# Row maxima of an attention kernel: transposed by VectorE in blocks of 32 and placed by eight small transfers, in place of a matmul and a copy; router fed from sums of both halves

## The reference

```python
# attention (4 heads of 64 channels, n = 1024 pixels)
xn  = group_norm(x, 32 groups) * gn_w + gn_b
q,k,v = split(qkv_w @ xn + qkv_b)
p   = softmax(q^T k / 8, over the keys);   x = x + proj_w @ (v p^T) + proj_b
# conditional convolution (8 experts)
rw  = sigmoid(mean_over_pixels(x) @ router_w.T + router_b)
W1,W2,W3 = sum_e rw[e] * experts_e         # 1x1, 3x3, 1x1
y = relu(bn1(conv1(x))); y = relu(bn2(conv2(y))); out = relu(bn3(conv3(y)) + x)
```

## Time and profile before

| | |
|---|---|
| median of 3 runs | 1910.57 us (1909.94 to 1910.65) |
| the profiled execution, its own time | 1913.63 us |
| its span, first to last instruction | 1911.8 us |
| mean granted TensorE clock | 0.993 of full speed |
| busy: PE / PEld / DVE / ACT / POOL | 97% / 55% / 54% / 57% / 75% |
| packets of all DMAs under 512 B | 26112 of 96673 |

### The profile page before, as it was taken

One profiled execution on the slowest core, in us unless ns is written; L12 is line 12 of the kernel. 1 busy time (PEld: TensorE's weight loads), 2 busy tenths in 40 slices (PEclk: granted clock), 3 DMA queues, 4 the chain that ended last, 5 costly groups with the idle time before them and its releaser, 6 DMA issues.

```text
span 1911.8 us, 29495 instructions
## 1 busy us (share of the span) xinstructions
PE 1846.7 (97%) x8332; PEld 1061.0 (55%) x8332; DVE 1041.8 (54%) x1820; ACT 1084.0 (57%) x1501; POOL 1438.7 (75%) x829
## 2 busy tenths in 40 slices
PE   6899999999999999999999999999999999999986
PEld 4455556555555555555555555555555555565532
DVE  6656556464654646555464654646556465564514
ACT  4455646556465555756556565565655556465452
POOL 3677968778796886968778687786968879687582
PEclk9999999999999999999999999999999999999998
DMA  3022423314233233332324233233332324222233
GB/s 114 27 56 67 117 79 89 96 56 121 88 94 85 65 106 89 105 89 74 100 64 122 76 91 94 65 107 94 94 95 72 89 83 118 76 84 78 64 107 99
DMA packets 96673, 166.72 MB, mean 87 GB/s; under 512 B 26112, under 2 KB 26880, under 8 KB 96640
## 3 DMA queue, kind: packets, MB, share of 16 engines
q1 hardware_dynamic: 96640, 166.31, 30.5%
HBM read 97.41 MB, written 17.04 MB: 60 GB/s over the span
## 4 chain that ended last, share of the span: by engine, by line
PE 87%; DVE 5%; issue 3%; POOL 2%; ACT 2%; DMA 0%; DVEq 0%; SPq 0%; POOLq 0%; ACTq 0%
PE PV L790 23%; PE R L627 14%; PE S L772 12%; PE R L754 11%; PE S L775 10%; PE R L678 5%; PE R L717 4%; DVE mx L994 3%; PE R L670 2%; POOL psum_p L601 2%; PE R L725 2%; PE R L701 1%; PE R L683 1%; DVE K L1015 1%; ACT K L883 1%
## 5 line engine op out<-in xcount | busy, mean ns | idle before, releaser
L601 POOL TENSOR_TENSOR psum_p<-psum_p,prob 128x1024 f32<-128x1024 f32 x384 | 915.7, 2385 | 305.8 <-ACT prob L868 286.6
L994 DVE TENSOR_REDUCE mx<-R 128x1 f32<-128x512 f32 x1006 | 653.5, 683 | 582.6 <-PE R L754 575.5
L868 ACT ACTIVATE prob<-S 128x1024 f32<-128x1024 f32 x512 | 518.3, 1022 | 319.2 <-PE S L775 316.3
L790 PE MATMUL PV<-prob,V 128*64 128x512 f32 x2048 | 469.4, 600 | 0.0
L772 PE MATMUL S<-Q,K 128*128 128x512 f32 x1024 | 445.1, 435 | 2.5 <-ACT prob L868 2.5
L775 PE MATMUL S<-Q,K 128*128 128x512 f32 x1024 | 403.2, 394 | 2.4 <-DMA Q<-mrow 2.4
L754 PE MATMUL R<-K,Q 128*128 128x512 f32 x1006 | 336.5, 405 | 13.1 <-DVE mx L994 7.9
L790 PEld LDWEIGHTS PV<-prob,V 128*64 128x64 f32 x2048 | 135.9, 137 | 254.8 <-issue 239.3
L772 PEld LDWEIGHTS S<-Q,K 128*128 128x128 f32 x1024 | 192.9, 188 | 131.5 <-issue 82.1
L754 PEld LDWEIGHTS R<-K,Q 128*128 128x128 f32 x1006 | 186.0, 187 | 94.1 <-DVE mx L994 49.0
L775 PEld LDWEIGHTS S<-Q,K 128*128 128x128 f32 x1024 | 193.5, 189 | 47.1 <-issue 14.4
(11 more groups left out here) (158 smaller groups left out, 1780.3 us busy)
## 6 DMA issues: line engine op xcount, KB each, us to landing
ex<-in_experts_dram SPq DMA_DIRECT2D x122, 352.0 KB, 3.3
xin<-in_x_dram SPq DMA_DIRECT2D x64, 256.0 KB, 3.2
K<-K SPq DMA_DIRECT2D x128, 128.0 KB, 2.3
Q<-Q SPq DMA_DIRECT2D x128, 128.0 KB, 2.3
x<-in_x_dram SPq DMA_DIRECT2D x64, 256.0 KB, 3.7
rz<-z_dram SPq DMA_DIRECT2D x126, 128.0 KB, 2.9
out_dram<-y SPq DMA_DIRECT2D x63, 256.0 KB, 2.7
V<-v_next SPq DMA_DIRECT2D x16, 512.0 KB, 3.8
```

The source lines that it names most:

```text
L601: nc.gpsimd.tensor_tensor(acc, first_in, prob[:, s % PBUF, :, :], ALU.add).then_inc(add_done, 1)
L790: last = nc.tensor.matmul(PV[own(a), :], V[:, b // NH, kt, a * D:a * D + D], prob[:, s % PBUF, a, :], start=(kt == 0), stop=(kt == KT - 1))
L868: nc.scalar.activation(prob[:, s % PBUF, :, :], S[:, s % 2, :, :], ACT.Exp, scale=D ** -0.5).then_inc(exp_done, 1)
L994: nc.vector.reduce_max(mx[:, b % 2, nh, m:m + 1], R[:, fill_bank(b, m, nh), :], AX.X).then_inc(max_read, 1)
```

## The change

Per block, the matmul, its PSUM bank and the copy are gone. VectorE's `max_of_block` now goes on itself: it writes the eight maxima into the first eight columns of mx1 (now 128 x 32, the rest zeros), waits for that, and transposes each block of 32 x 32 into mxt. The maxima of queries 32g to 32g+31 of query tile t then lie on partition 32g+t, so SP places them with eight DMAs a block (four groups g for each of two heads), each of four pieces of 32 numbers. The sign moves into K2, which holds minus ones. SP's `rows` moves from the tables of jobs to LOADS, at the end of n = 2, 10, 18 and 26, where before it stood at the start of n = 3, 11, 19 and 27. Two banks of FILL_BANKS at n = 8 are swapped. For the router VectorE adds the two halves into pool2 after the last projection, and the router is two matmuls in place of four.

```diff
-    PLACES ... 3: [("row", 0, 1)], 11: [("row", 0, 2)], 27: [("row", 1, 0)];  EARLY 19: [("row", 0, 3), ("v", 1, 2)]
+    PLACES, EARLY: the same without row
-LOADS = {3: [("v1", 0, 0)], 14: [("xin", 2, 0)], ...
+LOADS = {2: [("row", 0, 1)], 3: [("v1", 0, 0)], 10: [("row", 0, 2)], 14: [("xin", 2, 0)], 16: [("xin", 2, 1)], 18: [("row", 0, 3)],
+         19: [("xin", 2, 2), ("xin", 2, 3)], 22: [("h", -1, 0)], 26: [("row", 1, 0)]}
...
-        mx1 = sb("mx1", [P, 2 * QT])
-        mrow = sb("mrow", [2 * QT, P], F32R)
+        mx1 = sb("mx1", [P, ZP])
+        mxt = sb("mxt", [P, ZP])
...
             def rows(i, b):
-                sp.wait_ge(read["row"], BLOCKS * i + b + 1)
+                sp.wait_ge(max_turned, BLOCKS * i + b + 1)
                 for a in range(2):
                     r = 64 - 64 * a
-                    sp.dma_start(Q2[r:r + 1, 2 * p + a, px(hf)].bitcast(F32),
-                                 mrow[QT * a:QT * a + QT, :].bitcast(F32)).then_inc(rows_loaded, 16)
+                    for g in range(QT):
+                        sp.dma_start(Q2[r:r + 1, 2 * p + a, px(hf)].rearrange("o (t g c) -> o g t c", t=QT, g=QT)[:, g, :, :].bitcast(F32),
+                                     mxt[ZP * g + QT * a:ZP * g + QT * a + QT, :]).then_inc(rows_loaded, 16)
...
-                fills += [(K2[r:r + 1, h, :].bitcast(F32), 1.0)]
+                fills += [(K2[r:r + 1, h, :].bitcast(F32), -1.0)]
...
-                elif kind == "row":
-                    pe.wait_ge(max_ready, BLOCKS * i + f + 1)
-                    last = nc.tensor.matmul(bank[0:2 * QT, 0:P], mx1[:, :], negeye[:, :], start=True, stop=True)
...
                 elif kind == "router":
-                    pe.wait_ge(read["proj"], 4 * i + 4)
+                    pe.wait_ge(pooled, i + 1)
                     for c in range(CC):
-                        for hf in range(NH):
-                            last = nc.tensor.matmul(bank[:, 0:E], pool4[:, c, hf:hf + 1].to_broadcast([P, P]), wr[:, c, :],
-                                                    start=(c + hf == 0), stop=(c + hf == CC + NH - 2))
+                        last = nc.tensor.matmul(bank[:, 0:E], pool2[:, c:c + 1].to_broadcast([P, P]), wr[:, c, :], start=(c == 0), stop=(c == CC - 1))
...
             def max_of_block(i, b):
                 dve.wait_ge(max_read, 2 * (32 * i + 8 * b + 8))
-                wait(dve, filled["row"], BLOCKS * i + b)
-                nc.vector.reduce_max(mx1[:, :], mx[:, b % 2, :, :].rearrange("p n m -> p m n"), AX.X).then_inc(max_ready, 1)
-            def row(i, b, bank):
-                wait(dve, rows_loaded, 32 * (BLOCKS * i + b))
-                nc.vector.tensor_copy(mrow[:, :], bank[0:2 * QT, 0:P]).then_inc(read["row"], 1)
+                wait(dve, max_turned, BLOCKS * i + b)
+                nc.vector.reduce_max(mx1[:, 0:2 * QT], mx[:, b % 2, :, :].rearrange("p n m -> p m n"), AX.X).then_inc(max_ready, 1)
+                dve.wait_ge(max_ready, BLOCKS * i + b + 1)
+                wait(dve, rows_loaded, 16 * 2 * QT * (BLOCKS * i + b))
+                nc.vector.transpose(mxt[:, :], mx1[:, :]).then_inc(max_turned, 1)
...
                                                    accum_out=pool4[:, oc, hf:hf + 1]).then_inc(read["proj"], 1)
+                    if f == 3:
+                        dve.wait_ge(read["proj"], 4 * i + 4)
+                        nc.vector.reduce_sum(pool2[:, :], pool4[:, :, :], AX.X).then_inc(pooled, 1)
```

More of the change, by code:

```diff
@@ L72 @@
 TURNS = STEPS // BATCH
[L73 to L76, removed]
+PLACES = {2: [("proj", -1, 0)], 4: [("gna", 1, 0)], 6: [("proj", -1, 1)], 7: [("qk", 0, 7), ("gnb", 1, 0)], 8: [("proj", -1, 2)],
[3 rows of a table added]
 HALVES = {3: [("z", 0, 0)], 4: [("z", 0, 1), ("conv1", -1, 0)], 5: [("conv2a", -1, 0), ("conv2", -1, 0), ("z", 0, 2)],
           6: [("conv3", -1, 0), ("conv3", -1, 1)], 7: [("conv3", -1, 2), ("conv3", -1, 3), ("z", 0, 3)]}
-BANK_OF = {"qk": (1, 1, 2, 1, 2, 2, 2, 0), "v": (0, 2, 0, 1, 0, 1, 1, 2), "row": (1, 2, 1, 1), "proj": (2, 0, 1, 1), "gna": (2,),
-           "gnb": (1,), "router": (1,), "conv1": (0,), "conv2": (2,), "z": (0, 2, 0, 1), "conv3": (1, 2, 2, 0)}
-FILL_BANKS = ((0, 1), (0, 1), (0, 1), (0, 1), (0, 1), (2, 0), (1, 2), (1, 2), (2, 0), (0, 2), (0, 2), (0, 2), (2, 1), (2, 0), (0, 2), (0, 2),
+BANK_OF = {"qk": (1, 1, 2, 1, 2, 2, 2, 0), "v": (0, 2, 0, 1, 0, 1, 1, 2), "proj": (2, 0, 1, 1), "gna": (2,), "gnb": (1,),
+           "router": (1,), "conv1": (0,), "conv2": (2,), "z": (0, 2, 0, 1), "conv3": (1, 2, 2, 0)}
+FILL_BANKS = ((0, 1), (0, 1), (0, 1), (0, 1), (0, 1), (2, 0), (1, 2), (1, 2), (0, 2), (0, 2), (0, 2), (0, 2), (2, 1), (2, 0), (0, 2), (0, 2),
               (2, 0), (2, 1), (0, 1), (2, 1), (1, 2), (2, 0), (0, 2), (0, 2), (1, 2), (2, 0), (0, 2), (0, 2), (1, 0), (0, 1), (0, 1), (0, 1))
-EARLY = {0: [("qk", 0, 6)], 19: [("row", 0, 3), ("v", 1, 2)], 31: [("qk", 1, 5)]}
+EARLY = {0: [("qk", 0, 6)], 19: [("v", 1, 2)], 31: [("qk", 1, 5)]}
 PROLOGUE = [("gna", 0, 0), ("gnb", 0, 0)] + [("qk", 0, f) for f in range(4)] + [("v", 0, f) for f in range(8)] + [("bias", 0, 0), ("qk", 0, 4), ("qk", 0, 5)]
@@ L96 @@
 FIRST_PAIRS = 8 + AHEAD - len(EXTRA)
[L99 to L106, removed]
+WORK = {1: [("low", 0, 12)], 3: [("low", 0, 13)], 5: [("proj", -1, 0), ("stats", 1, 0)], 7: [("stats", 1, 1), ("recip", -1, 3)],
+        8: [("gna", 1, 0)], 13: [("proj", -1, 1)], 15: [("gnb", 1, 0), ("low", 0, 14), ("low", 0, 15)], 17: [("proj", -1, 2)],
+        19: [("proj", -1, 3)], 21: [("router", -1, 0)], 22: [("gates", -1, 0)], 27: [("low", 1, 0)], 29: [("low", 1, 1)],
+        31: [("low", 1, 2), ("low", 1, 3), ("low", 1, 4), ("low", 1, 5)], 38: [("recip", 0, 0)], 46: [("low", 1, 6), ("low", 1, 7)],
+        52: [("recip", 0, 1)], 53: [("recip", 0, 2)], 55: [("conv3", -1, 0), ("conv3", -1, 1)], 59: [("low", 1, 8), ("low", 1, 9)],
+        61: [("low", 1, 10)], 62: [("low", 1, 11)], 63: [("conv3", -1, 2), ("conv3", -1, 3)]}
 ACT_WORK = {7: [("normal", 1, 0)], 9: [("normal", 1, 1)], 10: [("product", -1, 0), ("product", -1, 1)],
@@ L117, with build @@
              31: [("norm", 0, 2)]}
-LOADS = {3: [("v1", 0, 0)], 14: [("xin", 2, 0)], 16: [("xin", 2, 1)], 19: [("xin", 2, 2), ("xin", 2, 3)], 22: [("h", -1, 0)]}
-def build(nc, x, vecs, router_b, wqkv, wproj, wrouter, experts, neg_eye, group_avg, out):
+LOADS = {2: [("row", 0, 1)], 3: [("v1", 0, 0)], 10: [("row", 0, 2)], 14: [("xin", 2, 0)], 16: [("xin", 2, 1)], 18: [("row", 0, 3)],
+         19: [("xin", 2, 2), ("xin", 2, 3)], 22: [("h", -1, 0)], 26: [("row", 1, 0)]}
+def build(nc, x, vecs, router_b, wqkv, wproj, wrouter, experts, group_avg, out):
     ctx = ExitStack()
@@ L247, in build @@
         max_ready = sem("max_ready")
-        filled = {k: sem(k + "_filled") for k in ("qk", "v", "z", "proj", "gna", "gnb", "router", "conv1", "conv2", "conv3", "row", "bias")}
+        max_turned = sem("max_turned")
+        pooled = sem("pooled")
+        filled = {k: sem(k + "_filled") for k in ("qk", "v", "z", "proj", "gna", "gnb", "router", "conv1", "conv2", "conv3", "bias")}
         qk_hi = sem("qk_hi")
         qk_lo = sem("qk_lo")
-        read = {"qk": qk_lo} | {k: sem(k + "_read") for k in ("v", "z", "proj", "gna", "gnb", "router", "conv1", "conv2", "conv3", "row", "bias")}
-        per_image = {"bias": 1, "row": BLOCKS, "qk": 8, "v": 8, "z": 4, "proj": 4, "gna": 1, "gnb": 1, "router": 1, "conv1": 1, "conv2": 1, "conv3": 4}
+        read = {"qk": qk_lo} | {k: sem(k + "_read") for k in ("v", "z", "proj", "gna", "gnb", "router", "conv1", "conv2", "conv3", "bias")}
+        per_image = {"bias": 1, "qk": 8, "v": 8, "z": 4, "proj": 4, "gna": 1, "gnb": 1, "router": 1, "conv1": 1, "conv2": 1, "conv3": 4}
         stats_ready = sem("stats_ready")
@@ L442, in section @@
                             dup(i + di, f)
-                        if kind == "row":
-                            rows(i + di, f)
                     if last and n == 18:
@@ L469, in section @@
                     for kind, di, f in LOADS.get(n, []):
+                        if kind == "row" and in_range(di, first, last):
+                            rows(i + di, f)
                         if kind == "xin" and more:
@@ L569, in split_x @@
                                         ALU.subtract).then_inc(xsplit_ready, 1)
-            for dst, value in ((neghalf[:, :], -0.5), (var_scale[:, :], SUBSETS / N), (var_eps[:, :], EPS), (mx[:, :, :, :], -3.0e38)):
+            for dst, value in ((neghalf[:, :], -0.5), (var_scale[:, :], SUBSETS / N), (var_eps[:, :], EPS), (mx[:, :, :, :], -3.0e38), (mx1[:, :], 0.0)):
                 nc.gpsimd.memset(dst, value).then_inc(consts_set, 1)
-            pool.wait_ge(consts_set, 4)
+            pool.wait_ge(consts_set, 5)
             pool.wait_ge(norm_loaded, 16)
@@ L576, in _ @@
             affine(0)
-            count = 4
+            count = 5
             fills = [(ones[:, :], 1.0), (hpad[:, :], 0.0)]
@@ L809, in _ @@
```

(6 more changed lines are left out.)

16 lines of the change are left out of this document (7 added, 9 removed), and 3 rows, old and new, of the table PLACES.

## The result

The median after is 1925.2 us (1923.5 to 1926.5, six runs) against 1910.3 us (1908.6 to 1913.2, six runs) before: a ratio of 1.0072, with 1.0062 to 1.0082 as its 95% interval. The forecast was 1929 us with a range of 1890 to 1945. The span of the profiled execution grew from 1911.8 to 1924.4 us, by 12.6 us, of which the sum had promised 17.9.

The account below looks back on a forecast made before the run. The prediction took TensorE to bound the kernel. Block 0 stalls +19.5, block 1 -5.1, router to hrow +4.2 and -0.8, relief -3.0, prologue +3.3 and final router -0.2 gave +17.9 us: 1929 us, range 1890 to 1945.

Parts of the forecast that it names:

- What bounds the kernel: TensorE: 87% of the chain of waits lies on it and it is busy for 97% of the span.
- the new stall at n = 30: TensorE waits 1.6 us for the next image's block 0 rows, 1.3 us later than before, in 15 images.
- The run of eight: SP's eight row issues a block take 5.2 us, so rows leave 3.86 us later than with two.
- The landing: After the end of a block's last row issue, TensorE resumes 1.07 us later.
- Rivals 1 and 2: SP's run takes 3.3 us, total 1884 us (chance 0.18); or 4.8 us, total 1911 to 1917 (chance 0.11).
- These three savings are eaten, and the place is 0.3 us later than before: At TensorE's hrow matmul: savings of 0.35, 0.32 and 0.50 us are lost waiting for the second hrow issue.
- rival 3: Each n = 30 stall drops TensorE's clock, costing 2.9 us an image on top: 1972 us; chance 0.05.
- Savings of TensorE: 0.32 us a block without the row matmul, 0.50 at step 19, 0.35 at the router; busy time falls about 28.
- The relief: While TensorE waits at n = 30, VectorE finishes K parts needed at n = 31: 0.2 us back an image.
- Image 0: First image up to its n = 30 stall, no router or convolution yet: 1.3 us saved.
- Prologue: Before image 0's first score: first row issue at 39.2, TensorE resumes at 45.4 against 42.14, +3.3 us.
- The last image: Its stretch from router to hrow was put at 0 us; last image and end together at -0.5 us.

Follow-up runs that it names:

- experiment 7: The changed kernel with block 0's eight row issues put ahead of the last exchange of softmax sums in SP's queue: 1902.7 us.
- experiment 2: The changed kernel with the router's part undone (four matmuls from both halves, no sum by VectorE): 1932.6 us.
- experiment 8: The changed kernel with the hrow copies issued at n = 19, ahead of two image loads, in place of n = 22: 1908.3 us.
- experiment 3: The kernel before, with six more transfers a block into a tile nobody reads, for which TensorE also waits: 1985.8 us.
- experiment 6: The changed kernel with four transposes and two transfers a block, each transfer of sixteen pieces of 128 bytes: 1883.4 us.
- experiment 5: The changed kernel with four 32 x 32 transposes side by side and two transfers a block, of four 512-byte rows each: 1883.4 us.
- experiment 4: The changed kernel with only block 1's transpose moved later, to where the old copy stood: 1975.2 us.

## Why the prediction was right, step by step

The sum missed by 5.3 us, by terms that go both ways: -0.8 in the prologue, -3.0 in image 0 with its stall, -2.8 in the inner images, +1.3 at the end. That 1929 came so near to 1925 is partly luck.

**What bounds the kernel, and the new stall at n = 30: right.** It was said to be 1.6 us in 15 images, 1.3 later than before. It is 1.2 to 1.6 in thirteen, 2.6 and 2.0 in the other two. The place in the queue did it, not the table entry: experiment 7 changes only that place and wins 22 us.

**The run of eight: 5.2 us forecast, 5.0 to 5.1 measured.** The forecast took every start 0.64 us after the last; the first two distances are 0.71 and 0.67 and the others 0.62 (medians). The landing, 1.07 forecast, is 1.05. Rivals 1 and 2 needed runs of 4.7 and 4.8. The 2.0 us per DMA that the prediction quotes from the Trainium skill ("DMA: Bandwidth & Descriptors", Anatomy of one DMA) stand there in a section on transfers issued by GpSimd. These are issued by SP, and from the start of the last issue to TensorE's release it is 1.62 us (0.57 + 1.05).

**"These three savings are eaten, and the place is 0.3 us later than before": the step that failed, by cancelling errors.** I had the second hrow issue 1.9 us later than before, since the expert loads and POOL's mixing would slip by 0.3 and two runs would push it. Against the image's first score it did not move (90.2): the run of eight is 3.7 us longer, but POOL's chain comes 1.2 us earlier, as experiment 2 shows, and the gap of 2.4 us in SP's queue took the rest. And I had 4.0 us for the landing. The second issue, for which TensorE waits, takes 4.7 to 5.4 in the thirteen images that wait, and 4.0 before. With the gap gone it follows the image loads closely: in one image (the ninth) the last load lands 1.7 us before that issue starts in the kernel before and 1.4 us after it starts in after. Issued ahead of the loads (experiment 8) it lands in 4.1 again. So the queue costs a second time, in the landing.

Together TensorE gets past hrow 0.1 to 0.8 us earlier than before against the image's first score, 0.5 on the mean (all but the image of rival 3 below), where the forecast comes to 0.2 (0.20 + 0.32 - 0.3). So of the 1.74 us saved up to there (0.17 + 0.31 + 0.45 + 0.31 + 0.50) the wait eats about 1.3. The row belongs to the tile hrow, min/median/max from issue to landing, both issues of all images:

```profile
DMA to landing us min/median/max: 3.2/4.7/5.4
```

**Savings of TensorE: right.** 0.31 for 0.32 and 0.50 for 0.50; the router 0.45 for 0.35. TensorE's busy time fell by 26.2 us for "about 28". The relief was 0.17 for 0.2. The 0.46 us that the prediction reads for a fill stands in neither of rows 2 and 3, but the 0.23 that it draws from it holds: at step 19 the score matmuls start 0.23 us apart (1142.41 and 1142.64).

**Image 0: -1.3 forecast up to its stall, -5.7 measured.** The forecast took the row matmul of block 1 at 0.32 us there too. Before, it waited for VectorE, and the pv matmuls behind it ran slowly (timeline of TensorE and a stretch with its granted clock, the last number but two; first before, then after):

```profile
61.61 0.38 PE L683 MATMUL R<-negeye,mx 128*8 128x128 f32 x2 [1.09 <-DVE mx L1002]
61.92 5.35 PE L790 MATMUL PV<-prob,V 128*64 128x512 f32 x16
...
62.00:65.40 3.40, 3.40 (x10) 0.96 (x12) 0.84 (x3) 0.00 (x0) 0.00 (x0) 0.50 0.02 8
```

```profile
61.46 3.65 PE L785 MATMUL PV<-prob,V 128*64 128x512 f32 x16
...
61.40:65.10 3.70, 3.70 (x18) 1.11 (x17) 2.41 (x6) 0.00 (x0) 0.76 (x1) 1.00 0.00 0
```

Without the matmul the wait goes (1.09), the 0.32 goes, and sixteen pv matmuls take 3.65 us instead of 5.35, as they do in the inner images: the clock was at its 1.2 GHz level (0.50) there and is at the full one after. That is 3.1 us in one place, and TensorE's timeline of image 0 before shows both the wait and the slow matmuls. The forecast took a row of the inner images for image 0.

**Prologue: +3.3 forecast, +2.5.** The first issue starts at 38.53 and not at 39.2: the matmul and the copy had taken more than the 0.5 us that I allowed. SP and TensorE there, and the clock behind it:

```profile
38.53 5.08 SPq L408 DMA_DIRECT2D Q<-mxt  x8
...
44.65 0.80 PE L770 MATMUL S<-Q,K 128*128 128x512 f32 x1 [6.03 <-DMA Q<-mxt]
```

```profile
44.60:47.00 2.40, 2.35 (x6) 1.86 (x7) 0.00 (x0) 0.58 (x1) 0.00 (x0) 0.50 0.81 188
47.00:49.00 2.00, 2.00 (x9) 1.55 (x8) 0.00 (x0) 1.56 (x3) 0.00 (x1) 0.87 0.89 283
```

The 1.2 GHz level lasts until about 47.3 us; before, it lasted until 48.3. TensorE works 2.7 us at that level instead of 6.2, and gets 1.5 us back by n = 3. The remaining 1.1 us of image 0's difference are the smaller steps behind its n = 6.

**Rival 3, the clock, had a part of the truth.** It was given for all 15 stalls and came behind one. After the stall of 2.04 us in one image the granted clock was 0.71, after the usual ones 1.00:

```profile
960.20:962.90 2.70, 2.65 (x11) 2.17 (x12) 2.03 (x3) 1.29 (x2) 2.58 (x2) 1.00 0.73 230
...
1193.30:1196.00 2.70, 2.62 (x8) 2.16 (x9) 1.36 (x3) 1.02 (x1) 2.42 (x2) 0.71 0.76 231
```

That image is 1.5 us longer than its neighbours. The term would be 1.5 us a drop, not the 2.9 that I took.

**The last image** gained nothing: the stretch that I had put at 0 ends 0.8 us later. TensorE comes to the first convolution ahead of before, but waits there for POOL's mixing, 0.7 us longer, and behind this wait the granted clock is 0.51, the 1.2 GHz level, where before it was 1.00. The eight matmuls take 3.6 us in place of 1.9 (timelines and stretches, first before, then after):

```profile
1838.77 1.94 PE L701 MATMUL R<-x,mix 128*64 128x512 f32 x8 [2.58 <-POOL mix L557]
...
1838.80:1842.20 3.40, 3.40 (x15) 1.81 (x16) 0.00 (x0) 1.44 (x2) 3.26 (x2) 1.00 0.58 174
```

```profile
1849.70 3.63 PE L696 MATMUL R<-x,mix 128*64 128x512 f32 x8 [3.32 <-POOL mix L558]
...
1849.70:1853.10 3.40, 3.40 (x8) 0.85 (x8) 0.00 (x0) 0.00 (x0) 3.26 (x2) 0.51 0.59 173
```

## What to carry to other kernels

A change that removes work from the busiest engine and adds issues to an idle queue is priced at the queue's ordered places: for each thing that is waited for, compare start of its issue + issues ahead of it + landing with the time at which it is asked for. SP was far from full (its issues fill 43% of the span after, 32% before), and two places an image still turned a gain of 27 us into a loss of 15. And ask what stands between "the data are ready" and "the queue may send them": here the same eight issues cost 50 us more when the transpose came 5 us after the maxima, and the inner images nothing when they and hrow stood earlier in the queue.

## What the runs showed of the hardware

- Issues from SBUF to SBUF on SP's queue, medians by their place in a run: the first 0.67 us, the second 0.62, the third to eighth 0.57, one every 0.62 us. It is the same for four pieces of 128 bytes (after) and of 512 bytes (experiment 3). With sixteen pieces of 128 bytes (experiment 6) the first takes 0.74 and the second 0.69. Short pieces had no cost in the end: the kernel of experiment 6 moves 128-byte pieces and takes the time of experiment 5.
- A transpose by VectorE of 128 x 32 f32 takes 211 ns, of 32 x 32 takes 200 ns: splitting it in four costs 0.6 us and lets the result lie on 32 partitions. The Trainium skill ("VectorE: DVE Perf Modes", The three transpose paths) says that blocks of 32 x 32 are transposed independently within a bank; experiment 5 shows that the block may be written to other partitions than the 32 it was read from.
- The clock after a stall, counted over after and experiments 3 and 4: of 41 stalls of 0.8 to 1.7 us (all at n = 30) none was followed by a lower granted clock; of 32 between 2.0 and 2.6 us thirteen were, at 0.50 to 0.76 over the next 2.7 us, with 1.3 to 1.7 us lost over the next five steps (0.6 in two of them, both in image 1). A short stall is not always free: in image 0 before, stalls of 0.91, 1.31 and 1.09 us come within 6 us, and the clock is 0.50 behind the third; after has the first two (0.90 and 1.30) without the third, and the clock stays at 1.00. What decides is open.
